# Up-bias inside the weights, other first loads, and a reciprocal built from ln and exp

## The reference

```
# RWKV mixer: k, v, r are projections of x mixed with the previous token
wkv[t] = (e1*aa[t-1] + e2*v[t]) / (e1*bb[t-1] + e2)    # aa, bb: running sums with decay
out    = (sigmoid(r) * wkv) @ Wo.T
# MoE 0 (8 experts, 2 per token, hidden 344): silu(x@Wg) * (x@Wu) @ Wd
# MoE 1 (8 experts, 2 per token, hidden 512), x here is z:
h   = silu(z @ we1[e] + be1[e])
out = h @ we2[e] + be2[e]
```

## Time and profile before

| | |
|---|---|
| Median of 3 runs | 757.58 us (757.11 to 758.16) |
| Profiled execution | 756.79 us, its span 755.0 us |
| PE busy | 611.3 us |
| DVE, ACT, POOL busy | 420.4, 346.6, 395.7 us |

### The profile page before, as it was taken

One profiled execution on the slowest core, in us unless ns is written; L12 is line 12 of the kernel. 1 busy time (PEld: TensorE's weight loads), 2 busy tenths in 40 slices (PEclk: granted clock), 3 DMA queues, 4 the chain that ended last, 5 costly groups with the idle time before them and its releaser, 6 DMA issues.

```text
span 755.0 us, 13385 instructions
## 1 busy us (share of the span) xinstructions
PE 611.3 (81%) x4216; PEld 514.5 (68%) x4248; DVE 420.4 (56%) x1156; ACT 346.6 (46%) x661; POOL 395.7 (52%) x405
## 2 busy tenths in 40 slices
PE   1288996978478798898989879998678699988792
PEld 0288996757356797798879867664623279977782
DVE  6726225797849964654146054859899876232002
ACT  1154863763248464574775545231111234755351
POOL 3176787561577346767776774321000466267742
PEclk9998998999699998998999999999789699999897
DMA  8166213201322011332231231002000112114213
GB/s 344 33 196 195 57 39 100 43 16 43 89 53 34 15 56 52 97 80 43 79 108 41 53 107 36 22 12 69 1 11 17 26 40 46 49 44 135 51 33 101
DMA packets 42977, 50.28 MB, mean 67 GB/s; under 512 B 8352, under 2 KB 34336, under 8 KB 42912
## 3 DMA queue, kind: packets, MB, share of 16 engines
q0 software_dynamic: 11776, 24.14, 13.2%
q1 hardware_dynamic: 31136, 25.28, 10.3%
HBM read 32.09 MB, written 17.30 MB: 65 GB/s over the span
## 4 chain that ended last, share of the span: by engine, by line
PE 49%; DVE 17%; POOL 13%; issue 9%; DMA 8%; ACT 2%; SPq 1%; ACTq 0%; DVEq 0%; POOLq 0%
PE bank L587 12%; PE bank L565 9%; PE bank L574 8%; POOL xs L1020 7%; DMA xs<-tokens_in,idx_in 6%; PE bank L663 5%; POOL tokens_out L1030 4%; PE bank L691 4%; PE bank L546 2%; PE bank L511 2%; DVE mixer L1305 2%; PE bank L491 1%; PE bank L572 1%; DMA yg<-tokens_out 1%; DVE hT L1210 1%
## 5 line engine op out<-in xcount | busy, mean ns | idle before, releaser
L1030 POOL DMA_INDIRECT tokens_out<-ys,idx_out x184 | 189.9, 1032 | 179.8 <-ACT ys L850 140.3
L1020 POOL DMA_INDIRECT xs<-tokens_in,idx_in x184 | 180.1, 979 | 156.9 <-DVE owner L1190 80.3
L788 ACT ACTIVATE w_up<-w 128x728 f32 (+1 forms) x184 | 131.2, 718 | 136.6 <-PE bank L565 66.5
L587 PE MATMUL bank<-w,hT 128*128 x1288 | 181.5, 284 | 8.4 <-ACT ys L850 3.0
L587 PEld LDWEIGHTS bank<-w,hT 128*128 128x128 f32 x1288 | 163.4, 196 | 24.0 <-issue 22.6
L565 PE MATMUL bank<-xT_kept,w_up 128*128 128x128 f32 x1104 | 159.2, 296 | 8.3 <-DVE hT L1210 5.0
L565 PEld LDWEIGHTS bank<-xT_kept,w_up 128*128 128x128 f32 x1104 | 147.8, 209 | 16.5 <-DVE hT L1210 7.5
L1210 DVE TENSOR_TENSOR hT<-gate,bank 128x384 f32<-128x384 f32 x92 | 50.7, 551 | 101.6 <-PE bank L565 72.5
L1226 DVE SCALAR_TENSOR_TENSOR x<-yg,cw,x 128x128 f32<-128x128 f32 x128 | 37.4, 340 | 125.1 <-DMA yg<-tokens_out 125.0
L574 PEld LDWEIGHTS bank<-xT_kept,w_up 128*128 128x128 f32 x736 | 97.7, 193 | 7.4 <-issue 4.6
L574 PE MATMUL bank<-xT_kept,w_up 128*128 128x128 f32 x736 | 97.7, 276 | 6.1 <-issue 2.1
(11 more groups left out here) (166 smaller groups left out, 674.6 us busy)
## 6 DMA issues: line engine op xcount, KB each, us to landing
yg<-tokens_out SPq DMA_DIRECT2D x64, 128.0 KB, 2.7
w<-in_w SPq DMA_DIRECT2D x8, 536.0 KB, 9.6
tokens_in<-xn SPq DMA_DIRECT2D x16, 256.0 KB, 2.6
w<-in_w SPq DMA_DIRECT2D x8, 512.0 KB, 9.4
xs<-tokens_in,idx_in POOLq DMA_INDIRECT x184, 2.6
tokens_out<-ys,idx_out POOLq DMA_INDIRECT x184, 2.3
x<-in_x SPq DMA_DIRECT2D x2, 512.0 KB, 8.6
out<-x SPq DMA_DIRECT2D x8, 128.0 KB
```

The costliest lines, as they stand in the source:

```text
L587: last = mm(y, hT[0:n_f, n % 2, c * P:(c + 1) * P], w_of(k, e, WD[k] + c * P, P, n_f), start=(c == 0), stop=(k == 0 and c == CH[k] - 1))
L788: nc.scalar.activation(w_up[:, n % 3, 0:UP[k]], w_of(k, e, 0, UP[k]), ACT.Copy).then_inc(w_copied, 1)
L1020: pool.indirect_dma_start(xs[:, j % RING, :], None, xn_dram[b], tile_rows(idx_in, b, j))\
L1030: pool.indirect_dma_start(ys_dram[b], tile_rows(idx_out, b, j), ys[:, j % RING, :], None)\
```

## The change

**Up-bias.** L572, `bsel`, `unit` and PE's up registers are gone. For MoE 1 the normed tokens are stored in DRAM tensors of their own, 127 columns only; column 127 is filled once with ones (a store of single elements per sequence). `fold`, once, changes each expert's up-weights: row i becomes row i minus row 127 (PE multiplies with `less_last`, a matrix of identity minus last row, then ACT copies 127 rows back), and row 127 is then overwritten with be1 by one small load. So the ordinary product gives bias and all. The fold is 8 products of 128 x 512 f32 on PE and 8 copies on ACT; in both lists its steps stand one by one among those of the first RWKV window.

**First loads.** x of sequence 0 comes in two halves, each with its semaphore; DVE's and the table setups' waits for `const` move into the setups. Only 256 columns of `bconst_raw` come first; the selector's 1024 columns come behind the expert loads, and their copy on POOL stands ahead of the bias steps. The bias arrives in one load, 128 columns wide (before: 14 loads, 256 wide).

**RWKV.** The denominator's product and sum go from POOL to DVE. ACT makes inv = exp(-ln(den)), and DVE corrects it with one Newton step: (den*inv - 2)*inv = -1/den; the sign is taken back by -0.5 in the residual. ACT's list has, one behind the other, in the first window tanh 1, inverse 0, one fold copy, inverse 1; in the second tanh 1, inverse 0, a copy of transposed rows, inverse 1. In DVE's list: correction 0, both products of half 0, correction 1, a gate product, both products of half 1.

**Order.** All of `TURNS` except SP's later part is new. What the strings come to at the start: DVE has eight rows of statistics, two instructions on the identity for `less_last`, the root, the norm; `decay_setup` comes later, behind the norm after the first RWKV. On POOL:

| pass | gathers ahead of its first scatter, before | after |
|---|---|---|
| (0,0) | 12 | 23 |
| (3,0) | 16 | 23 |
| (5,1) | 8 | 16 |

From the first gather to the last scatter of (0,0) POOL's list has 56 transfers before and after (bias steps between: 2 of 3 before, all 3 after); of (3,0) 66 before, 64 after; from the first gather of (5,1) to the end 51 both, the last gather being the 39th before and the 32nd after. In the second retention, the routing of (5,0) stands four DVE steps earlier.

The diff, cut to its core:

```
 sync: rows(b)
-    sp.dma_start(by_token(xn_dram[b])[:, i * HT:(i + 1) * HT, :],
-                 xn[:, b, i * HT:(i + 1) * HT, :]).then_inc(st_xn[b], 16)
+    d = P - KIND[f]
+    sp.dma_start(by_token(xn_dram[KIND[f]][b])[:, i * HT:(i + 1) * HT, 0:d],
+                 xn[:, b, i * HT:(i + 1) * HT, 0:d]).then_inc(st_xn[b], 16)
 sync: later_loads()
+    sp.wait_ge(ones_made, 1)
+    for b in range(NB):
+        sp.dma_start(by_token(xn_dram[1][b])[:, :, P - 1:P], ones[:, :].unsqueeze(2),
+                     allow_slow_non_contiguous=True).then_inc(st_ones, 16)
+    yield
+    sp.wait_ge(FOLD_ACT.sem, FOLD_ACT.done(0, f"e{E - 1}"))
+    last_row = heads(w_all[1][P - 1:P, :], E, WIDE[1])
+    sp.dma_start(last_row[:, :, 0:F1], bias_in[0:E, 0:F1].unsqueeze(0)).then_inc(ld_be1, 16)
 sync: first loads
+    for i in range(NH):
+        sp.dma_start(x[:, i * HT:(i + 1) * HT, :], x_in[:, i * HT:(i + 1) * HT, :]).then_inc(ld_x0[i], 16)
     sp.dma_start(const[:, :], const_in).then_inc(ld_const, 16)
     sp.dma_start(colv[:, :], cols_in).then_inc(ld_const, 16)
+    sp.dma_start(bconst_raw[:, 0:B_SEL], bconst_in[:, 0:B_SEL]).then_inc(ld_bconst, 16)
     load_w(0)
+    sp.dma_start(bconst_raw[:, B_SEL:NBC], bconst_in[:, B_SEL:NBC]).then_inc(ld_sel, 16)
+    sp.dma_start(x[:, NT:2 * NT, :], x_in[:, NT:2 * NT, :]).then_inc(ld_x1, 16)
 tensor: project_up(p, j), MoE 1
-    e = owner_of(up_owner, j)
-    mm(to[:], bparts[:, 0:P], bsel[:, bass.ds(e, 1), :].rearrange("p a b -> p (a b)"), start=True, stop=False)
     for c in range(CH[k]):
         last = mm(to[:, c * P:(c + 1) * P], w_up[:, n % 3, c * P:(c + 1) * P], rows_in,
-                  start=False, stop=(c == CH[k] - 1))
+                  start=True, stop=True)
 tensor: fold()
+    for e in range(E):
+        yield
+        if e == 0:
+            pe.wait_ge(ld_w[1], 16 * E)
+            pe.wait_ge(less_made, 2)
+        to = take(CB[1] + e % 2, FOLD_ACT, 0, f"e{e}")
+        mm(to[:], less_last[:, :], w_of(1, e, 0, F1), start=True, stop=True).then_inc(FOLD_PE.sem, 1)
 scalar: fold()
+    for e in range(E):
+        yield
+        after(FOLD_PE, 0, f"e{e}")
+        run(w_of(1, e, 0, F1, P - 1), bank[CB[1] + e % 2][0:P - 1, :], ACT.Copy, FOLD_ACT)
 scalar: rwkv(b)
+    def inverse(i):
+        after(RW_DVE[b], 0, f"num{i}")
+        run(rw_ex[:, i, 3, :], rw_ex[:, i, 1, :], ACT.Ln, RW_INV[b])
+        after(RW_INV[b], 0, f"ln{i}")
+        run(rw_ex[:, i, 3, :], rw_ex[:, i, 3, :], ACT.Exp, RW_INV[b], scale=-1.0)
 gpsimd: bias_setup()
-    eye = ...; own_unit = ...            # unit: three tensor_tensor, one cast to bsel (128 x 4096)
+    step(nc.gpsimd.tensor_copy(bconst[:, B_SEL:NBC], bconst_raw[:, B_SEL:NBC]))   # with the first bias step
 gpsimd: rwkv(b)
-    nc.gpsimd.tensor_tensor(den, e1, rw_bb[:, i * HALF:(i + 1) * HALF], ALU.mult).then_inc(RW_POOL[b].sem, 1)
-    nc.gpsimd.tensor_tensor(den, den, e2, ALU.add).then_inc(RW_POOL[b].sem, 1)
 vector: rwkv_sums(b, i)
     step(V.tensor_tensor(num, e1, aa0, ALU.mult))
+    step(V.tensor_tensor(den, e1, bb0, ALU.mult))
     step(V.tensor_tensor(rw_t, e2, v, ALU.mult))
+    yield
+    after(RW_DVE[b], 0, f"d1{i}")
+    step(V.tensor_tensor(den, den, e2, ALU.add))
     after(RW_DVE[b], 0, f"n2{i}")
     step(V.tensor_tensor(num, num, rw_t, ALU.add))
 vector: rwkv_out(b, i)
-    after(RW_POOL[b], 0, f"den{i}")
-    step(V.reciprocal(den, den))
+    after(RW_INV[b], 0, f"inv{i}")
+    step(V.tensor_tensor(rec, den, inv, ALU.mult))
+    after(RW_DVE[b], 0, f"dr{i}")
+    step(V.scalar_tensor_tensor(rec, rec, -2.0, inv, ALU.add, ALU.mult))
 vector: less_last_row()
+    V.tensor_scalar(less_last[:, 0:P - 1], eye[:, 0:P - 1], eye[:, P - 1:P], None, ALU.subtract).then_inc(less_made, 1)
+    V.memset(less_last[:, P - 1:P], 0.0).then_inc(less_made, 1)
```

More of the change, by code:

```diff
@@ L159, in sem @@
             return ctx.enter_context(nc.semaphore(name))
-        xn_dram = [nc.dram_tensor(f"tokens_in{b}", [S, P], F32).ap() for b in range(NB)]
+        xn_dram = [[nc.dram_tensor(f"tokens_in{k}_{b}", [S, P], F32).ap() for b in range(NB)] for k in range(2)]
         ys_dram = [nc.dram_tensor(f"tokens_out{b}", [K * S + TILES * P, P], F32).ap() for b in range(NB)]
@@ L170, in build_block @@
         btri = sb("btri", [P, P], BF16)
-        bparts = sb("bparts", [P, 2 * P], BF16)
-        bsel = sb("bsel", [P, E, F1], BF16)
-        bias_raw = sb("bias_raw", [P, 2 * P])
-        bias_part = sb("bias_part", [P, 2 * P], BF16)
-        unit = sb("unit", [P, E * CH[1]])
+        bparts = sb("bparts", [P, P], BF16)
+        bias_raw = sb("bias_raw", [P, P])
+        bias_part = sb("bias_part", [P, P], BF16)
+        less_last = sb("less_last", [P, P])
+        ones = sb("ones", [P, NT])
         gn = sb("gn", [P, 2])
@@ L267, in build_block @@
         xT, ybank = bank[2:4]
-        ld_x = [sem(f"ld_x{b}") for b in range(NB)]
+        ld_x0 = [sem(f"ld_x0_{i}") for i in range(NH)]
+        ld_x1 = sem("ld_x1")
+        ld_sel = sem("ld_sel")
         ld_const = sem("ld_const")
@@ L352, in w_of @@
         def w_of(k, e, start, n, rows=P):
+            if isinstance(e, int):
+                return w_all[k][0:rows, e * WIDE[k] + start:e * WIDE[k] + start + n]
             view = heads(w_all[k][0:rows, :], E, WIDE[k])[:, bass.ds(e, 1), start:start + n]
@@ L467, in _ @@
             mm = nc.tensor.matmul
-            up_owner = [pe.alloc_register(f"up_owner{i}") for i in range(4)]
             down_owner = [pe.alloc_register(f"down_owner{i}") for i in range(4)]
@@ L589, in project_down @@
                 if k == 1:
-                    last = mm(y, bconst[:, bass.ds(e * P + B_SEL, P)], bparts[:, P:2 * P], start=False, stop=True)
+                    last = mm(y, bconst[:, bass.ds(e * P + B_SEL, P)], bparts[:, :], start=False, stop=True)
                 last.then_inc(down_done, 1)
@@ L619, in downs @@
                             after(RT_DVE[b], SUB[f], "te")
+                            if (f, b) == (3, 0):
+                                after(SETUP, 0, "b3")
                             load_owner(down_owner, b, 0)
@@ L722, in beside @@
                 yield from route(0, b)
+                if b == 1:
+                    yield from fold()
                 yield from norm(1, b)
@@ L884, in rwkv @@
                     gate_half(i)
+                for i in range(NH):
+                    yield
+                    inverse(i)
             def rope_table():
@@ L928, in _ @@
             nc.gpsimd.memset(xnT[:, :, 0:1], 0.0).then_inc(zero_kept, 1)
+            nc.gpsimd.memset(ones[:, :], 1.0).then_inc(ones_made, 1)
             def after(steps, rnd, name):
@@ L1031, in scatter @@
                         .then_inc(st_ys[j // 2 % (RING // 2)], 16)
-            def rwkv(b):
-                for i in range(NH):
-                    den, e1, e2 = (rw_ex[:, i, a, :] for a in range(1, 4))
-                    yield
-                    after(RW_DVE[b], 0, f"bb{i}")
-                    nc.gpsimd.tensor_tensor(den, e1, rw_bb[:, i * HALF:(i + 1) * HALF], ALU.mult).then_inc(RW_POOL[b].sem, 1)
-                    after(RW_POOL[b], 0, f"d1{i}")
-                    nc.gpsimd.tensor_tensor(den, den, e2, ALU.add).then_inc(RW_POOL[b].sem, 1)
             def rows_in(b):
-                yield from gather(0, b)
-                yield from rwkv(b)
-                for f in (2, 3, 5):
+                for f in KIND:
                     yield from gather(f, b)
@@ L1259, in rwkv_exponents @@
                 after(RW_SET, 0, "bb0")
+                after(SETUP, 0, "sel")
                 if b:
@@ L1302, in rwkv_out @@
                 wkv, den = (rw_ex[:, i, a, :] for a in range(2))
-                after(RW_POOL[b], 0, f"den{i}")
-                step(V.reciprocal(den, den))
+                after(RW_DVE[b], 0, f"den{i}")
+                rec, inv = (rw_ex[:, i, a, :] for a in range(2, 4))
+                after(RW_INV[b], 0, f"inv{i}")
+                step(V.tensor_tensor(rec, den, inv, ALU.mult))
+                after(RW_DVE[b], 0, f"dr{i}")
+                step(V.scalar_tensor_tensor(rec, rec, -2.0, inv, ALU.add, ALU.mult))
+                yield
                 after(RW_DVE[b], 0, f"rec{i}")
-                yield
-                step(V.tensor_tensor(wkv, wkv, den, ALU.mult))
+                step(V.tensor_tensor(wkv, wkv, rec, ALU.mult))
                 after(RW_DVE[b], 0, f"wkv{i}")
@@ L1421, in decay_setup @@
                 yield
+                dve.wait_ge(ld_const, 16 * 2)
                 step(V.memset(half, 0.5), "half")
```

92 lines of the change are left out of this document (44 added, 48 removed), and 62 rows, old and new, of the table TURNS.

## The result

The changed kernel took 736.69 us (median of 4 runs, 733.1 to 739.37) against 757.35 for the kernel before (4 runs): ratio 0.9736, 95% interval 0.9674 to 0.9797. In a second set, five runs of it beside eleven of the kernel before on one chip, it was 737.57 (734.82 to 742.7), ratio 0.973 [0.9698, 0.9763]. Forecast: 736, in a range of 723 to 751. The profiled execution is the slowest of the four, 739.37 us with a span of 737.5; before it was 755.0. So the trace shows 17.5 of the 20.7 us by which the medians differ.

What follows compares the result with a forecast made beforehand. No engine was taken to bound the whole (TensorE busy 81%); different engines fill different stretches. Terms summed to -21.7 from the profiled 756.79, giving 735.1; with the runs' median 0.8 above, 736 us, range 723 to 751.

Steps and rivals of the forecast that it cites:

- Start: To the root's first step: statistics wait for half the rows, POOL's selector cast gone; -6.3 us.
- First pair: First pair of passes: bias steps half as wide, -2.0 us; two stores of ones delay gathers, +1.0.
- the starved ring of the rivals: Gathers put first delay scatters, so y copies wait for the ring of 8; 769 us, chance 0.05.
- RWKV: First window: last gate product 2.7 us later after T (end of L1296's second run), less 0.5 won before: +2.2.
- In the second window the tile stream decides: 0: Second RWKV window: DVE's chain loses the same, but PE's tile stream sets the time; 0, bounds -2 and +2.2.
- one table for ln and exp: Rival: ln and exp share one ACT table, so no second and third load; 732 us, chance 0.2.
- (d): From second retention to the last pass's first gather: PE full, nine up-bias products gone; -1.9 us.
- (e): Last pass: last gather 32nd of 51 transfers instead of 39th, PE's last ten tiles shorter; -6.0 us.
- POOL's order gives nothing: Rival: gathers put ahead save nothing in pass (3,0) and the last pass; 745 us, chance 0.2.
- (a): Pass (3,0), first gather to last scatter: 64 transfers instead of 66, less PE work; -5.0 us, bounds 0 and 10.
- (b): First retention beside pass (3,1): PE full, 13 up-bias products gone; -2.7 us.
- (c): Second retention: DVE's stretch, with PE's part near its end; -1.0 us.

## Why the prediction was right, and which terms were not

**Start: right.** -6.9 for -6.3. With POOL's cast gone, the successor of the 3.27 us instruction takes 0.16, as the prediction had it; no run put the cast back by itself.

**First pair: right in sum.** Up to DVE's first RWKV scan -0.4 for -1.0, less than the 4 us by which executions differ there. The price of the ones (+1.0) was too high, as the run with the later stores shows. Within the pair the first pass became 3.1 us longer (first gather to last scatter 81.6, before 78.5; 79.3 to 81.6 in seven traces with the new order, 77.4 to 78.5 in three with the old) and what follows made it up. One place of it is in the chain that ended last, in order of time: POOL's bias steps and six gathers (79.8 to 93.6) stand ahead of a scatter, ACT's y copy waits for its landing, and PE for the copy:

```profile
93.85 1.00 POOL tokens_out L1062
...
95.16 2.27 DMA tokens_out<-ys,idx_out
97.50 0.39 ACT ys L874
...
98.05 1.47 PE bank L600 x6
```

That is the starved ring of the rivals, once and for 2.4 us of PE, not for 33. It is also the kind of wait, of down products for a y copy, that the prediction had listed as a sign of being wrong.

**RWKV: the loads right, the path wrong.** Four table loads for ln and exp and one for silu, as forecast; the inverses were ready at T + 6.9 and T + 11.3 (forecast 6.5 and 10.9), the last gate product at T + 15.3 (14.2). The first window lost 3.1 (34.8 to 37.9). But only 1.1 of it goes with ln and exp. The other 2.0 are there with the plain reciprocal too: up to T the window gained 0.7, and behind T it lost 2.7, 2.15 of them at a gate product that stands ahead of the reciprocal and whose up product comes late in PE's list. The sum had no term for that. Behind the window DVE's list has gate products of the other pass between the receptance product and the norm, and these came late; at the norm's root (L1117, 178.00, before 178.69) only 0.7 of the 7.3 us lead was left. In all the first RWKV cost 4.8 us, for 2.2.

"In the second window the tile stream decides: 0" is the step that failed. From its first scan to the first gather of (2,1) the change lost 3.7 us, and the same in five traces. The sum followed DVE's chain alone and took the tile stream as untouched, but ACT's block of loads stands ahead of the stream's copies and silus: PE waited up to 5.8 us for one y copy in the first window, and in the second stretch it idled 2.6 us longer and worked 2.4 us longer at a lower clock than with the reciprocal, for the same instructions. With the reciprocal the stretch takes 65.0 us (one trace), less than before the change (66.2), so ln and exp cost 5.0 there and the rest of the change gave 1.3. The stage behind, for which the sum had no term, grew by 1.7 (56.9; 56.3 with the reciprocal), mostly not by ln and exp; its cause stays open. From the first RWKV's first scan to the first gather of (3,0), all told, the change lost 8.6 us (204.1 to 212.7), for 2.2: the 4.8, 3.7 and 1.7 above, less 1.6 in the stretch between the two RWKVs. The rival "one table for ln and exp" is dead: the trace has a load ahead of each.

The Trainium skill (ScalarE: Activation LUTs, Table sets: the hidden batching unit) has ln then exp as one load; the trace has two, at 158.13 and 160.07. Its section What ACT_TABLE_LOAD costs has some 2.66 us for a switch with its drain; here the load takes the 1.28 us that the section has for it, but the next function starts 1.30 us after the load does, with no drain. The measurements decide on both.

**The up-bias: right.** The claim that 92 products of 0.21 are worth only what lies where PE ends last, about 8 us of 19, was tested both ways: 9.8 us taken away from the kernel before, 9.8 put into the changed one, each known to some 3 us, and neither near 19. Of the terms, (d) was too small: 3.5 and 3.0 alone, for 1.9.

**POOL's order: right in the last pass, wrong in the first MoE 1 pass.** (e) -7.2 for -6.0: the old order in the changed kernel loses 8.9 us there, the new order in the old kernel gains 7.6. These stages are of one trace each, but the times of the whole kernels (9 and 7.5 us) say the same. So the rival "POOL's order gives nothing" falls, but for (e) alone. In (a), -3.3 for -5.0, the prediction put the gain down to gathers put ahead and transfers moved out of the stretch; what the old order loses in (a), it gains back in (b). From the first gather of (3,0) to the last scatter of (3,1) the change gave 5.9 us (175.3 to 169.5), and by the two exchanges POOL's new order is worth 0.5 of that or costs 1.5. The bias product accounts for 4.2 of it by the one run and 2.9 by the other; the rest is PE's and ACT's new lists or chance, which wasn't taken apart. The ring isn't starved in MoE 1: PE's waits for y copies from the first MoE 1 gather on are 0.25, 0.25 and 0.58. (c) was -3.5 for -1.0. The bias product is worth 0.8 and 0.6 there, so most of the rest is something else, perhaps the routing of (5,0) four steps earlier; this wasn't tried.

**The sum.** The trace gives -17.5 for -21.7, mainly because RWKV and the stage behind it cost more than 2.2 and (c) gave 2.5 more than its term. The profiled execution is the slowest of four; the medians differ by 20.7, 1 us from the forecast of 736. That closeness is in part luck: the 6 us too few for RWKV were met by 3.7 too few in (c) and (e), and the profiled execution, on which the stages are read, was 2.7 us above its kernel's median.

## What to carry to other kernels

Before an instruction is moved to another engine, add up what the receiving engine does around it and what is queued behind it: here 3.34 us of DVE became two loads of 1.28, two functions of 0.6 and a wait, with two more instructions on DVE, and the plain reciprocal was faster by 5 us; grouped by function, the same ACT work was too (731.97 and 732.48 can't be told apart). An engine's list that only reorders transfers can be worth as much as removing work (7.6 and 8.9 us in the last pass), where its waits, and not its busy time, fill the stage and nothing behind the stage can give the time back; in the first MoE 1 pass the same kind of exchange moved some 5 us from one stage to the next and gained nothing. So add up neighbouring stages before a gain is put down to one. And count a stall at what it does to PE's clock as well as at its length: PE's busy time over the same instructions in one stretch shows it, where several traces agree; the total of one execution does not.

## What was not expected of the hardware

In the second RWKV's stretch the same 412 PE instructions took 59.0 to 59.3 us of busy time at a granted clock of 0.88 to 0.89 (five traces with ln, exp, ln, exp) and 56.9 at 0.94 with the reciprocal: of the 5.0 us between them about half is clock. Elsewhere the clock differs by as much between executions of one program: 0.68 to 0.83 in the 20 us behind the first gather of (2,0). On the third chip the same kernel before took 877.75 instead of 757 us. Why is not known: no trace was kept of it there, and in those of the other versions PE's weight loads stand for up to 10.3 us at a time with no cause shown.
